# Four-layer decoder on one core: the recurrent experts layer with group sums on ScalarE, weight pieces in portions, and a first state by twelve matmuls

## The reference, cut to what matters

```
h0 = hidden_states.mean(axis=1) @ ctx_w.T + ctx_b
xw = hidden_states @ gru_w_ih.T
def step(h, xw_t):                       # 100 steps, one after the other, G = 1024
    hw = h @ gru_w_hh.T
    xr, xz, xn = jnp.split(xw_t, 3, axis=-1)
    hr, hz, hnn = jnp.split(hw, 3, axis=-1)
    r = jax.nn.sigmoid(xr + hr)
    z = jax.nn.sigmoid(xz + hz)
    n = jnp.tanh(xn + r * hnn)
    h_new = (1.0 - z) * n + z * h
routing = l2norm(hs as (B, S, E=8, D=128))
expr = (hidden_states @ expr_w.T).reshape(B, S, E, D)
gram = einsum('bsed,bsfd->bsef', routing, routing)      # goes into one scalar penalty
num = sum(expr * routing, -1)
den = max(|expr|, eps) * max(|routing|, eps)
scores = (1 - num / den) * (1 + penalty)                # then top 2 of 8 experts per token
```

## Time and profile before

| what | value |
| --- | --- |
| median of 3 runs | 3145.64 us (3142.97 to 3148.93) |
| time of the profiled execution | 3167.93 us |
| its span in the trace | 3166.1 us |
| mean granted clock of TensorE | 0.960 of full |
| busy: PE / DVE / ACT / POOL | 2786.7 / 1784.5 / 694.7 / 291.2 us |
| chain that ended last | PE 49%, DVE 31%, issue 6%, ACT 6%, DMA 5%, SP's queue 2%, POOL 1% |

### The profile page before, as it was taken

How to read it: one execution, slowest core, us unless ns; L and a number is a source line. 1 busy time by engine, 2 the same in 40 slices (tenths; PEclk the granted TensorE clock), 3 DMA queues, 4 the chain that set the end, 5 groups by cost and what they waited for, 6 DMA issues and landing times.

```text
span 3166.1 us, 78551 instructions
## 1 busy us (share of the span) xinstructions
PE 2786.7 (88%) x32325; PEld 1799.1 (57%) x32325; DVE 1784.5 (56%) x5591; ACT 694.7 (22%) x1851; POOL 291.2 (9%) x681
## 2 busy tenths in 40 slices
PE   6888999899988999998988997888888888888887
PEld 4554456579765555554655664555555555555577
DVE  4545435421146666467466441477877778777743
ACT  2331133311122444310013431111111111111211
POOL 2112211020221000000211100000000000000111
PEclk9989989999998999999999998999999999999999
DMA  4000000079530000457111007311111111111176
GB/s 150 1 1 1 8 27 15 9 273 328 178 121 1 1 1 1 142 186 236 59 32 24 2 32 321 105 21 26 22 24 25 26 25 22 24 25 26 29 263 236
DMA packets 210667, 241.29 MB, mean 76 GB/s; under 512 B 152285, under 2 KB 178634, under 8 KB 199306
## 3 DMA queue, kind: packets, MB, share of 16 engines
q1 hardware_dynamic: 206446, 230.35, 23.0%
q0 software_dynamic: 3968, 7.56, 0.7%
HBM read 188.93 MB, written 56.21 MB: 77 GB/s over the span
## 4 chain that ended last, share of the span: by engine, by line
PE 49%; DVE 31%; issue 6%; ACT 6%; DMA 5%; SPq 2%; POOL 1%; DVEq 0%; POOLq 0%; ACTq 0%
PE banks L948 4%; PE banks L1323 4%; PE banks L641 4%; DVE arena L2387 3%; PE banks L1130 3%; PE banks L841 2%; PE banks L582 2%; PE banks L1194 2%; PE banks L1206 2%; PE banks L1369 2%; PE banks L970 2%; ACT arena L1719 2%; PE banks L988 1%; PE banks L994 1%; DMA arena<-whh 1%
## 5 line engine op out<-in xcount | busy, mean ns | idle before, releaser
L1323 PE MATMUL banks<-arena 128*32 128x384 bf16 x19200 | 834.6, 331 | 146.4 <-DVE arena L2350 139.6
L1323 PEld LDWEIGHTS banks<-arena 128*32 128x32 bf16 x19200 | 513.8, 98 | 464.9 <-DVE arena L2350 208.0
L1719 ACT ACTIVATE arena<-arena 128x64 f32<-128x64 f32 x200 | 51.3, 256 | 791.8 <-DVE arena L2392 762.3
L1130 PE MATMUL banks<-arena 128*128 128x400 f32 x512 | 176.9, 508 | 14.5 <-DMA arena<-hh 13.0
L641 PE MATMUL banks<-XNT,arena 128*128 128x400 f32 x384 | 149.9, 532 | 9.2 <-ACT XNT L1445 3.8
L948 PE MATMUL banks<-arena 128*100 128x256 f32 x512 | 138.7, 425 | 16.1 <-ACT XNT L1445 5.4
L1130 PEld LDWEIGHTS banks<-arena 128*128 128x128 f32 x512 | 98.3, 193 | 93.2 <-DMA arena<-hh 15.6
L2387 DVE STREAM_TRANSPOSE arena<-banks 128x384 f32<-128x384 f32 x200 | 112.0, 560 | 57.6 <-PE banks L1323 30.7
L1919 DVE TENSOR_REDUCE arena<-banks 100x4 f32<-100x1444 f32 x64 | 106.3, 1660 | 59.1 <-PE banks L794 58.9
L2671 POOL TENSOR_TENSOR rstd<-rstd 100x3 f32<-100x3 f32 (+1 forms) x120 | 23.3, 194 | 1250.8 <-DVE rstd L1874 1244.5
L841 PEld LDWEIGHTS banks<-arena 32*121 32x121 f32 x1536 | 101.1, 188 | 58.0 <-ACT arena L1545 35.7
(11 more groups left out here) (403 smaller groups left out, 4644.1 us busy)
## 6 DMA issues: line engine op xcount, KB each, us to landing
arena<-fc SPq DMA_DIRECT2D x22, 1024.0 KB, 4.8
arena<-pj SPq DMA_DIRECT2D x22, 1024.0 KB, 5.1
arena<-gu SPq DMA_DIRECT2D x21, 1024.0 KB, 5.0
whh_parts<-arena SPq DMA_DIRECT2D x32, 576.0 KB, 3.1
arena<-whh_parts SPq DMA_DIRECT2D x32, 576.0 KB, 14.7
arena<-whh SPq DMA_DIRECT2D x128, 96.0 KB, 3.2
arena<-dn SPq DMA_DIRECT2D x21, 512.0 KB, 4.1
xw<-arena SPq DMA_DIRECT2D x4, 2400.0 KB, 8.7
```

The costliest lines, as they stand in the source:

```text
L1130: last = nc.tensor.matmul(u[:, 0:HALF], w, x[:, half * HALF:(half + 1) * HALF], start=i == 0, stop=i == len(parts) - 1)
L1323: last = nc.tensor.matmul(banks[32 * j:32 * j + 32, 2 * c + i, 0:384], hs_tops[:, 1 - i, ub, :], whh[:, ub, j, c, part, :], start=opens an ...
L1719: nc.scalar.activation(rz[:, c], pre[:, c], ACT.Sigmoid).then_inc(sem["rz_done"], 1)
```

## The change

1. **Splits.** `load_split` issues one transfer of 128 partitions instead of four of 32.
2. **First state.** `cw` and `cb` are loaded in two plain transfers instead of twelve with short runs. `mean` is padded to 32 columns and becomes the stationary side: eight matmuls with 256 moving columns and four for the bias, each group of three into its own 32 partitions; DVE then transposes the result into the state.
3. **Order of the transfers.** Blocks 4, 5, 6 come first. The sixteen pieces of blocks 1, 2, 3 and 7 are issued two or three at a time behind each store of an expression tile. The inputs of steps 0 and 1 are loaded early, but for one cell (second batch group, first half) that is still being computed; DVE copies that cell from the staged gates.
4. **Places.** The temporaries of a step (`gates_T` and so on) move to lie just below the state; `xin` moves below the staged gates and into a constant that is no longer used.
5. **Lap work.** The sums over groups go to ACT: one activation of 128 columns with an accumulator for each group, `Copy` on DVE's products and `Square` directly on `expr` and `seen`, three or four behind each half step of steps 0 to 7. DVE only multiplies (`group_products`), in six batches after steps 0, 1, 2, 4, 5 and 6. Three semaphores are added between DVE and ACT, `multiplied`, `summed` and `squared`; `expr_used` is given later in the lap and `seen_used` earlier. The roots are made in two parts. `lap_placed` moves from step 8 to step 9, `rank_lap` on PE from before step 8 to before step 9, and `dots_of(0)` leaves the lap loop and the first lap's end; only the last lap's remains, behind the loop.
6. **ACT's loop.** The short loop now runs the first lap only; nine laps are a second loop with ten steps unrolled.

The diff, cut to its core:

```
-                for j in range(4):
-                    sp.dma_start(split_in[v % 2][32 * j:32 * j + 32], whh_rows[ub % 4, :, j, ub // 4, j_out, :]).then_inc(sem["l_split%d" % (v % 2)], 16)
+                sp.dma_start(split_in[v % 2], whh_rows[ub % 4, ub // 4, j_out]).then_inc(sem["l_split%d" % (v % 2)], 16)
...
-            for ub in range(8):
+            for j in range(4):
                 for kk in range(C):
-                    nc.tensor.matmul(u[:, ub * B:(ub + 1) * B], cw[:, kk, ub, :], mean[:, kk, :],
+                    nc.tensor.matmul(u[32 * j:32 * j + 32, 0:256], mean[:, kk, :], cw[:, kk, 256 * j:256 * j + 256],
                                      start=kk == 0, stop=False, skip_group_check=True)
-                last = nc.tensor.matmul(u[:, ub * B:(ub + 1) * B], cb[:, ub, :], ones[0:1, 0:B], start=False, stop=True, skip_group_check=True)
+                last = nc.tensor.matmul(u[32 * j:32 * j + 32, 0:256], ones8, cb[0:1, 256 * j:256 * j + 256],
+                                        start=False, stop=True, skip_group_check=True)
...
-                rank_lap(lap, 4)
                 for i in range(2):
                     step_of(i, 2 * LAP * lap + 2 * (LAP - 2) + 2 * i)
+                    if i == 0:
+                        rank_lap(lap, 4)
...
+            def squares_of(x, first, some):
+                for e in some:
+                    last = nc.scalar.activation(unread[:, e % 4], x[:, e * ED:(e + 1) * ED], ACT.Square, accum_out=square_sums[:, first + e:first + e + 1])
+                return last
+
+            def group_sums(q, c, lap):
+                if c == 0:
+                    act.wait_ge(sem["multiplied"], len(distances) * lap + (q + 1 - len(distances)))
+                sums = [cross_sums[:, e:e + 1] if s_ == 0 else gram_sums[:, s_ + e * (E + 1):s_ + e * (E + 1) + 1]
+                        for s_ in distances[q] for e in range(E - s_)]
+                half = (len(sums) + 1) // 2
+                for m in (range(half), range(half, len(sums)))[c]:
+                    last = nc.scalar.activation(unread[:, m % half], prod[1 - q % 2][:, m * ED:(m + 1) * ED], ACT.Copy, accum_out=sums[m])
+                if c == 1:
+                    last.then_inc(sem["summed"], 1)
...
+            with act.Fori(1, LAPS) as lap:
+                for k in range(LAP):
+                    for c in range(2):
+                        half_of(k % 2, c, lambda a, b_: (a * LAP // 2) * lap + (a * (k // 2) + b_))
+                        lap_sums(k, c, lap)
...
+            n.wait("a_evac", n.got("a_evac"))
+            for i in range(2):
+                nc.vector.tensor_copy(xin[i][:, 1, 0], staged[0][:, :, :, i]).then_inc(sem["l_x%d" % i], 16)
             settle()
-            dve.wait_ge(sem["xw1"], 32)
...
+            def group_products(q, lap):
+                dve.wait_ge(sem["summed"], len(distances) * lap + (q - 1))
+                at_ = 0
+                for s_ in distances[q]:
+                    m = (E - s_) * ED
+                    last = nc.vector.tensor_tensor(prod[1 - q % 2][:, at_:at_ + m], expr if s_ == 0 else seen[:, 0:m], seen[:, s_ * ED:], ALU.mult)
+                    at_ += m
+                last.then_inc(sem["multiplied"], 1)
...
```

SP's list:

```
-            load_whh((1, 4, 5, 6))
+            load_whh((4, 5, 6))
...
-            load_whh((2, 3))
-            sp.wait_ge(sem["xw0"], 32)
-            load_whh((7,))
+            late = [(ub, j) for ub in (1, 2, 3, 7) for j in range(4)]
             for i in range(TILES):
...
                 sp.dma_start(shown[i * P:i * P + rows], expr_out[0:rows, i % 2]).then_inc(sem["e_out%d" % (i % 2)], 16)
+                for ub, j in late[16 * i // TILES:16 * (i + 1) // TILES]:
+                    if (ub, j) == (7, 0):
+                        sp.wait_ge(sem["xw0"], 32)
+                        sp.wait_ge(sem["xw1"], 16)
+                        for k in range(2):
+                            load_x(k, k, cells=((0, 0), (0, 1), (1, 1)))
+                    load_whh_part(ub, j)
```

More of the change, by code:

```diff
@@ L1713, in _, with half_of @@
             nc.scalar.preload_act_table(ACT.Sigmoid)
-            with act.Fori(0, S // 2) as t:
+            def half_of(i, c, at_):
+                k = 2 * i + c + 1
+                act.wait_ge(sem["pre"], at_(4, k))
+                nc.scalar.activation(rz[:, c], pre[:, c], ACT.Sigmoid).then_inc(sem["rz_done"], 1)
+                nc.scalar.activation(omz[:, c], pre[:, c, 4:8], ACT.Sigmoid, scale=-1.0)
+                act.wait_ge(sem["n_in"], at_(4, k))
+                nc.scalar.activation(cand[:, c], t1[:, c], ACT.Tanh).then_inc(sem["n_done"], 1)
@@ new lines, in lap_sums @@
+            def lap_sums(k, c, lap):
+                some = range(4 * c, 4 * c + 4)
+                if k == 0:
+                    if c == 0:
+                        act.wait_ge(sem["l_expr"], 160 * lap)
+                    squares_of(expr, E, some)
+                if k == 1:
+                    if c == 0:
+                        act.wait_ge(sem["l_seen"], 16 * lap)
+                    last = squares_of(seen, 0, some)
+                    if c == 1:
+                        last.then_inc(sem["squared"], 1)
+                if 2 <= k < 8:
+                    group_sums(k - 2, c, lap)
@@ L1715, in _ @@
+            with act.Fori(0, LAP // 2) as t:
                 for i in range(2):
                     for c in range(2):
[L1717 to L1720, removed]
-                        act.wait_ge(sem["n_in"], 4 * t + k)
-                        nc.scalar.activation(cand[:, c], t1[:, c], ACT.Tanh).then_inc(sem["n_done"], 1)
+                        half_of(i, c, lambda a, b_: a * t + b_)
@@ L2334, in _ @@
             n.wait("a_evac", n.got("a_evac"))
+            step(nc.vector.memset(mean[:, :, :], 0.0))
             for kk in range(C):
-                last = nc.vector.tensor_reduce(mean[:, kk, :], XNT[:, kk, :].rearrange("p (b s) -> p b s", b=B), AX, ALU.add)
+                last = nc.vector.tensor_reduce(mean[:, kk, 0:B], XNT[:, kk, :].rearrange("p (b s) -> p b s", b=B), AX, ALU.add)
             step(last)
@@ L2354, in _ @@
             input_gates(range(1, 12, 2))
[L2355 removed]
+            emptied(nc.vector.transpose(hs[:, 1].rearrange("p u r -> p (u r)"), take()[:, 0:256]))
             own()
@@ L2526, in _ @@
                 settled()
-            dve.wait_ge(sem["l_expr"], 160)
-            dots_of(0, slice(0, 1), 0)
+            dve.wait_ge(sem["xw1"], 32)
             lap_tables()
+            nc.vector.memset(gram_sums, 0.0)
+            nc.vector.memset(idle[:, 1:2], 0.0).then_inc(sem["summed"], len(distances))
             settled()
@@ L2543, in _ @@
+                        nc.vector.memset(idle[:, 1:2], 0.0).then_inc(sem["expr_used"], 1)
+                        first_roots(squares)
+                        group_products(2, lap)
                     if k == 3:
-                        scores_of(chunk)
-                        dots_of(8, chunk, 0)
+                        last_roots(squares)
                     if k == 4:
+                        inverses_of(chunk)
+                        group_products(3, lap)
+                    if k == 5:
+                        dve.wait_ge(sem["summed"], len(distances) * lap + 2)
+                        scores_from(cross_sums.rearrange("p (o e) -> p o e", o=1))
+                        group_products(4, lap)
@@ L2556, in _ @@
[L2556 to L2560 removed]
                     if k == 8:
[L2562 removed]
+                        dve.wait_ge(sem["summed"], len(distances) * lap + len(distances))
+                        nc.vector.tensor_copy(gram[:, chunk, :], gram_sums.rearrange("p (o q) -> p o q", o=1))
```

129 lines of the change are left out of this document (69 added, 60 removed).

## The result

The kernel after the change takes 3118.62 us in the median (3108.89 to 3146.02, 20 runs), where the kernel before, on the same chips, takes 3150.44 (3139.36 to 3166.61, 20 runs). The ratio is 0.9906, 95% interval 0.9885 to 0.9927. So it is faster by about 30 us, a third of the 91.5 that were forecast, and outside the range of 3028 to 3090.

A forecast was written before the change was run, and what follows sets the result against it. Bounds: DVE work beyond its slack per recurrence step, SP's rounds in the splits, DMA before the recurrence. Savings 8 + 24.5 + 2 + 57 = 91.5 us, from 3145.6 to 3054 us; range 3028 to 3090.

The forecast's parts named there:

- Splits: Layer 3's hidden-layer matmuls: one transfer per load shortens SP's rounds and PE's waits, saving 8 us, range 0 to 17.
- Order of the transfers: Stretch before the recurrence: pieces behind expression stores let the first step start at 1977, saving 24.5 us, range 10 to 27.
- First state: Before the expression tiles: twelve matmuls take at most 5.8 us, saving 4 us or more, worth nothing by itself.
- First inputs and the first two steps: Recurrence start: step 0 no longer waits 2.01 us for inputs, saving 2 us; 2.5 us in the next step left uncounted.
- Lap work: Recurrence laps: excess per lap falls from 11.35 to 5.2 us, saving 57 us with the ends of laps 0 and 9.
- DVE's excess: Laps: DVE work beyond about 2.1 us free per step lengthens it, only behind steps 2, 4, 6 and 9.
- ACT's sums: Half-step slots in the laps: four sums take 1.4 to 2.2 us, hidden in ACT's 2.30 us of idle time.
- B: Before the recurrence: tiles chain through store latency or block 0 lands late; stretch gives 10, splits 2: 3075 us; 17%.
- A: ACT in the recurrence: Copy and Square need table loads of 1.28 us, costing 101 us, so 3155 us; 3%.
- C: Laps: issue time replaces DVE's work and step 0 stays cold, 9 x 3 = 28 us less gain: 3083 us; 14%.

The follow-up runs named there:

- plain rows: Changed kernel, but weights laid out block by block so each split load is one transfer of 128 contiguous rows: 3073.1 us, ratio to before 0.9717.
- four loads: Changed kernel with only the split load undone, again four transfers of 32 partitions per block: 3083.2 us, ratio to before 0.9739.

## Why the prediction was right or wrong

- **Splits: wrong, and the step that failed.** The prediction gave the load a value between "nothing, if bytes and descriptors alone count" and 1.9 us of issue saved, so it let the edit only gain. It never bounded the loss, though no row of before showed a pattern with four groups of rows. The count of rows was the same, the number of engines that share them was not. The term of -8 measured +50.4. What the runs showed in its place: with 4 outermost some four DMA engines carry the load, its packets take 5.3 us in place of 2.1, and DVE, SP's rounds and at last PE wait for it. With a good pattern the edit gains, as forecast: with 128 rows the stretch is 11.7 us shorter than before, and SP's rounds are 13.9 us, where 14.3 was forecast.
- **Order of the transfers: right in mechanism, mis-sized.** 16.8 us and not 24.5. The sum of bytes had 26.5 MB; the trace moved 396 GB/s x 73.9 us = 29.3 MB. It had left out a store of staged gates of 2.46 MB that is issued just ahead of `ew`, 6 us at that rate, and the rate was a little below the 404 to 415 assumed. That isn't the whole error, though: with 2.31 MB less the stretch still takes 70.95 us, where the prediction had 66 (1911 to 1977), since the first tiles then go at PE's pace.
- **First state: right that it is worth nothing by itself.** It takes 6.1 us and not "at most 5.8", 3.5 less than before and not "4 us or more", and is worth nothing once the pieces stand ahead again.
- **First inputs and the first two steps: better than forecast.** Step 0 has no wait on `xw` any more. Together with the end of lap 0 the difference is 8.3 us against 4.2. PE's gap of 5.35 us before the second step did not shrink to 3.3, it went altogether, and with it the fall of the clock behind it that made this step 10.53 us long: the 2.5 us that I did not count came on top, and more.
- **Lap work: right.** 92.25 us a lap against 92.8, 58.2 us in laps 1 to 9 against 54.5, step 9 at 11.6. DVE's excess lies behind steps 4, 6 and 9, as told, but not behind step 2, where it was told too (8.77 us there). Step 0 stays on the low clock in most laps, 9.85 us in the median. ACT's sums are hidden with half of their cover to spare.
- **Rivals.** B is half there (the evacuations of the last five tiles wait for a store, and the stretch gives 17 and not 24.5). A and C did not happen; C's 9 x 3 is 27 and not 28, which changes nothing. The real miss was no rival at all: nowhere was the single transfer slower. Without that one term the rest sums to 83.5 forecast and 83.3 measured, but that it agrees so closely is luck: 7.7 us too little from the order of the transfers are made up by 4.1 too much from the first steps and 3.7 from the laps.

## What to carry to other kernels

When transfers are merged, compare the outermost dimension of both patterns before and after, not only bytes and rows: in this stretch four transfers of 32 rows beat one of 4 by 32, and one of 128 rows beats both. For an edit whose form no row of the trace shows, keep a bound on the losing side even where it looks like pure saving. And when work is moved to fill slack, look for the place that also shortens PE's longest gap: here the gain was then the work's own time and the clock's.

## What the runs showed of the hardware

- **Engines per transfer.** With an outermost dimension of 4 or 8, 3.4 and 6.5 DMA engines work at once, with 16 or more 10 to 11 (table above).
- **The clock after a gap.** At the lap starts gaps of PE of 1.4 to 1.8 us left the granted clock at 1.00 in all eight laps. Gaps of 2.1 to 2.6 us brought it down in seven of eight, for instance to 0.55 in the 3 us behind that of 2.59, worth 1.3 us in the step there. The length of the gap doesn't settle it alone. Before the change the gaps at the lap starts were 3.4 to 4.2 us, and three of nine (3.90 to 3.95 us) left the clock at 1.00; so did the gap of 2.67 us before the first step after the change. What else decides it stays open.
- **The clock without a gap.** In layer 4's attention the granted clock fell while PE was busy 95% of the time, at different places in the two executions compared here. The windows view of the kernel with plain rows, and of the one with four loads; the first window of each starts at the same place of unchanged code, 25.9 us apart, and the second ends at about the same place:

```profile
1704.00:1734.00 30.00, 28.59 (x300) 19.59 (x296) 13.83 (x17) 11.35 (x19) 0.00 (x0) 0.83 0.01 2
...
1794.00:1845.00 51.00, 45.71 (x516) 32.85 (x512) 20.58 (x25) 15.79 (x26) 0.00 (x0) 0.76 0.01 1
```

```profile
1730.00:1760.00 30.00, 28.59 (x338) 19.90 (x339) 15.48 (x18) 13.76 (x23) 0.00 (x0) 1.00 0.01 2
...
1820.00:1860.00 40.00, 34.71 (x384) 24.99 (x380) 18.72 (x21) 15.06 (x25) 0.00 (x0) 0.87 0.01 1
```

In the first window PE did 300 matmuls in the one and 338 in the other. Its waits in that code agree in both kernels line by line to 0.3 us, so what the plain rows lost there is the clock: 11.0 us between two single profiles of unchanged code. Why the clock falls there stays open.
- **The loop's return.** DVE's 3.1 to 3.4 us of issue at the return of the unrolled body are there in the rows of all three forms: with the squares behind step 9, with the placing there, and with nothing there.
